# One-hots and weighing of the joined graph-attention stage: two calls a tile pair with two SBUF operands each, or a call per tile with one SBUF operand and a scalar per partition

## The chip, the cores and the metric

The kernel runs on one core of a Trainium2 chip. The metric is the device time of one execution in microseconds (us). About 0.2% (9.4 us) is what a measurement of this kernel can tell from no change.

## The reference, cut to what matters

The model is a node network of 3125 nodes and 53125 edges: an attention layer with 8 heads, a routed expert layer, a graph-attention network of three layers, and a second routed expert layer. The change touches the three graph-attention layers alone. Each does, with 4 heads of 128 columns (layers 1 and 2) or one head of 256 columns (layer 3):

```python
h = (x @ W).reshape(n, heads, out_ch)
e = jax.nn.leaky_relu(al_s[src] + al_d[dst], 0.2)
emax = jax.ops.segment_max(e, dst, num_segments=n)
ee = jnp.exp(e - emax[dst])
denom = jax.ops.segment_sum(ee, dst, num_segments=n)
alpha = ee / (denom[dst] + 1e-16)
out = jax.ops.segment_sum(h[src] * alpha[:, :, None], dst, num_segments=n)
```

## The kernel before

Edges are sorted by destination and cut into 232 items (`ITEMS`) of two tiles of 128 edges, an edge a partition. All edges of an item lead to one tile of 128 nodes. `phase_gat_layer` works on one layer; its engines run written-out loops over the items, in order, and wait on semaphores for each other. For item `t`:

- GpSimd (POOL, L1780) issues two indirect DMAs that gather the rows `h[src]` of the two tiles into slot `t % RING` of `g.rows`. `RING` is 12 slots in layers 1 and 2 and 24 in layer 3. Once the ring is full, an issue waits until item `t - RING` is summed.
- VectorE in `weigh(t)` makes the one-hots `hot` of the destinations (L2022, every fourth item, for four items at once) and multiplies head 0 of the gathered rows by its softmax numerators in `sums(t)` (L2028). In layer 3 head 0 is the whole row.
- ScalarE in `scale(t)` copies the weights beside the row (L1874) and multiplies heads 1 to 3 (L1880, six calls; none in layer 3).
- TensorE in `sum_item(t)` multiplies the one-hots with the rows (L1795) into a bank of PSUM: four matmuls of 261 columns in layers 1 and 2, two of 259 in layer 3. The profile keeps two records of each, so 8 an item and 4.
- VectorE in `add(t - LAG)` adds the bank to the node tile in `acc` (L2051). LAG is 2 in layers 1 and 2 and 5 in layer 3.

Beside this runs the softmax of the next chunk of 64 items (`CH`). For the first 44 items of a chunk three of four also carry `products(q)` on TensorE (L1812, L1815) and `take_scores(q)` on VectorE (L1926, L1930, L1934), as long as there are pairs left: this holds for items 0 to 43, 64 to 107 and 128 to about 155, 116 items in all (the stretches with scores, below). On the last 20 items of a chunk run the 20 steps of `softmax_step`, where TensorE and VectorE take turns. The last 40 items have neither. VectorE's order in a turn is: `weigh(t)`, `take_scores`, a softmax step, `add(t - LAG)`. The order is that of the code; no scheduler moves it.

`sum_item(t)` waits for `marked` (the one-hots), `weighed`, `scaled` and `added` of the bank. Between two gathers GpSimd has a gap that the profile calls issue. At the start of a chunk VectorE rescales `acc` (L2036: `tensor_scalar` with a scalar per partition, in place, on 128 columns in layers 1 and 2 and 256 in layer 3), and at the start of the program it makes `ident` and `before` (L252, L253: `tensor_scalar` on `iota_row` with a scalar per partition).

Of the kernel before, what the change touches and what calls it, by code (L numbers as in the profile page):

```python
# [22 lines left out]
ALU = mybir.AluOpType  # L23
# [3 lines left out]
P = 128  # L27
# [1660 lines left out]
def phase_gat_layer(k, g, s):  # L1688
# [14 lines left out]
    BATCH, HOTS, NB = 4, 3, 4  # L1703
# [22 lines left out]
    with Phase(k, f"gat{g.n}_layer") as ph:  # L1726
# [5 lines left out]
        hot = ph.sb("hot", [P, HOTS, 2 * BATCH, P])  # L1732
# [20 lines left out]

        def heads(t, h0, h1):
            return g.rows[:, t % RING, :, h0 * D:h1 * D].rearrange("p s (h d) -> p s h d", d=D)

        def sums(t):
            return g.sums[:, t // CH % 2, 2 * (t % CH):2 * (t % CH) + 2, :]
# [26 lines left out]
        def _(pe):  # L1785
            def sum_item(t):
                if t % BATCH == 0:
                    pe.wait_ge(marked, t // BATCH + 1)
                pe.wait_ge(weighed, t + 1)
                pe.wait_ge(scaled, t + 1)  # L1790
                if t >= S:
                    pe.wait_ge(added, t - S + 1)
                for p in range(PIECES):
                    for e in range(2):
                        mm = nc.tensor.matmul(k.ps[t % S * PIECES + p][:, 0:PIECE], hot[:, t // BATCH % HOTS, t % BATCH * 2 + e, :],  # L1795
                                              g.rows[:, t % RING, e, p * PIECE:(p + 1) * PIECE], start=(e == 0), stop=(e == 1))
                mm.then_inc(summed, 1)
# [111 lines left out]
        def _(dve):  # L1909
# [106 lines left out]
            def weigh(t):  # L2016
                if t % CH == 0:
                    dve.wait_ge(exped, t // CH + 1)
                if t % BATCH == 0:
                    if t >= HOTS * BATCH:  # L2020
                        dve.wait_ge(summed, t - (HOTS - 1) * BATCH)
                    v.tensor_tensor(hot[:, t // BATCH % HOTS],  # L2022
                                    k.iota_row[:, 0:P].rearrange("p (a n) -> p a n", a=1).to_broadcast([P, 2 * BATCH, P]),
                                    k.dst_in[:, 2 * t:2 * (t + BATCH)].rearrange("p (s a) -> p s a", a=1).to_broadcast([P, 2 * BATCH, P]),
                                    ALU.is_equal).then_inc(marked, 1)
                dve.wait_ge(gathered[t % RING], (t // RING + 1) * 32)
                alpha = sums(t)[:, :, 0:by_dve].rearrange("p s (h o) -> p s h o", o=1)
                v.tensor_tensor(heads(t, 0, by_dve), heads(t, 0, by_dve), alpha.to_broadcast([P, 2, by_dve, D]), ALU.mult  # L2028
                                ).then_inc(weighed, 1)
# [240 lines left out]
```

## Time and profile before

| | |
|---|---|
| median of 3 runs | 4693.39 us (4689.03 to 4693.57) |
| the profiled execution's own time | 4692.36 us |
| its span in the trace | 4690.3 us |
| item loop of layer 1 | 1798 to 2396 us of the span |
| item loop of layer 2 | 2618 to 3216 us |
| item loop of layer 3 | 3389 to 3968 us |
| busy over the span | PE 78%, DVE 58%, ACT 43%, POOL 46% |

The profile is of one execution; its span starts with the first instruction. PE is TensorE, PEld its weight loads, DVE VectorE, ACT ScalarE, POOL GpSimd. The three item loops hold 1775 us, 38% of the span, and only there the changed lines run.

### The profile page before, as it was taken

Reading aid. Unit: us, or ns where it says so; the run is one execution under the profiler, and the core shown is the slowest. Engines: PE = TensorE matmul, PEld = TensorE weight load, DVE = VectorE, ACT = ScalarE, POOL = GpSimd, SP = SyncE. Lnnn points to the kernel's source line nnn. Section 1 sums busy time; section 2 is a strip of 40 time slices with the busy share of each in tenths; the row PEclk is TensorE's granted clock in tenths of the full one; section 3 lists DMA queues with packets and bytes.
Section 4 is the critical chain, followed back from the end, with each engine's and each line's share of the span. In section 5 each row is a group of like instructions: output and inputs, shape, how many; then the busy total and the mean of one; then the engine's idle time right before and its main releaser. Section 6 shows DMA issues by size and latency. Waiting matters only on the chain. (4 is left out here: it accounts for less than half of the span.)

```text
span 4690.3 us, 76158 instructions
## 1 busy us (share of the span) xinstructions
PE 3671.9 (78%) x19902; PEld 2874.6 (61%) x19903; DVE 2735.7 (58%) x6769; ACT 2023.4 (43%) x6613; POOL 2138.2 (46%) x2124
## 2 busy tenths in 40 slices
PE   5788887896999467889768788976677666669995
PEld 3455554785888446677545667755555443458885
DVE  4688888444111458787656878766676655741112
ACT  0588884221222027788743778774311000212221
POOL 0577773001222015777721577772377775012221
PEclk9899998987999788999989899998787666869998
DMA  2677773444778646787643678764555433035555
GB/s 78 186 232 228 231 229 93 152 126 162 260 263 262 163 178 230 243 261 229 195 153 128 234 240 268 229 199 151 171 170 171 132 99 110 10 125 180 187 183 161
DMA packets 348560, 856.05 MB, mean 183 GB/s; under 512 B 52869, under 2 KB 156908, under 8 KB 339692
## 3 DMA queue, kind: packets, MB, share of 16 engines
q0 software_dynamic: 145920, 459.41, 32.6%
q1 hardware_dynamic: 202348, 393.24, 25.2%
q8 instruction: 123, 2.02, 0.2%
q14 instruction: 169, 1.38, 0.1%
HBM read 768.84 MB, written 83.63 MB: 182 GB/s over the span
## 5 line engine op out<-in xcount | busy, mean ns | idle before, releaser
L1780 POOL DMA_INDIRECT h<-h_table,src_of x1392 | 1424.3, 1023 | 954.9 <-PE ps L1815 461.7
L1795 PE MATMUL ps<-h,gat_layer_hot 128*128 128x261 f32 (+1 forms) x4640 | 1308.5, 429 | 372.8 <-DVE h L2028 264.0
L1795 PEld LDWEIGHTS ps<-h,gat_layer_hot 128*128 128x128 f32 x4640 | 910.5, 208 | 644.6 <-DVE gat_layer_hot L2022 208.0
L1880 ACT ACTIVATE h<-h,gat_shared 128x128 f32<-128x128 f32 x2784 | 863.0, 389 | 113.2 <-DMA h<-h_table,src_of 112.8
L727 POOL DMA_INDIRECT edges_rows<-kv_table,src_of x464 | 456.6, 984 | 269.5 <-POOLq L209 128.6
L2051 DVE TENSOR_TENSOR acc<-acc,ps 128x522 f32 (+1 forms) x696 | 421.9, 606 | 238.4 <-issue 105.8
L1012 ACT ACTIVATE acc<-ps,moe_experts_b 128x256 f32<-128x256 f32 x512 | 215.0, 471 | 690.4 <-PE ps L962 690.4
L962 PE MATMUL ps<-moe_experts_turned,moe_experts_w 128*128 128x256 f32 x2048 | 455.4, 381 | 0.0
L2028 DVE TENSOR_TENSOR h<-h,gat_shared 128x256 f32<-128x256 f32 (+1 forms) x696 | 354.7, 510 | 171.3 <-DMA h<-h_table,src_of 169.9
L973 PE MATMUL ps<-moe_experts_w,acc 128*128 128x256 f32 x2048 | 452.1, 379 | 0.0
L973 PEld LDWEIGHTS ps<-moe_experts_w,acc 128*128 128x128 f32 x2048 | 389.1, 190 | 52.9
L962 PEld LDWEIGHTS ps<-moe_experts_turned,moe_experts_w 128*128 128x128 f32 x2048 | 387.1, 191 | 50.5
L1413 POOL DMA_INDIRECT picked_out<-moe_experts_result,moe_slot_out x128 | 125.2, 978 | 635.7 <-DVE moe_experts_result L1390 616.1
L1406 POOL DMA_INDIRECT moe_experts_rows<-normed,moe_slot_in x128 | 124.2, 970 | 630.5 <-POOLq L209 570.2
L791 PE MATMUL ps<-edges_out_rows,h 128*128 128x264 f32 x928 | 280.3, 428 | 86.8 <-DVE edges_out_rows L826 85.1
L1390 DVE TENSOR_TENSOR moe_experts_result<-ps,moe_experts_b 128x512 f32<-128x512 f32 x64 | 44.3, 692 | 483.7 <-PE ps L973 483.7
L1865 ACT COPY gat_layer_of_item<-gat_layer_parts 128x24 bf16 (+1 forms) x696 | 145.7, 218 | 368.8 <-PE ps L1815 183.0
L781 PE MATMUL ps<-h 128*128 x928 | 271.3, 419 | 22.1 <-ACT h L745 13.0
L1812 PE MATMUL ps<-gat_layer_parts,gat_layer_hots 128*128 128x100 bf16 (+1 forms) x4176 | 229.1, 204 | 75.5 <-DMA gat_layer_hots<-hot_table 40.3
L1812 PEld LDWEIGHTS ps<-gat_layer_parts,gat_layer_hots 128*128 128x128 bf16 x4176 | 209.7, 103 | 127.5 <-issue 71.2
L791 PEld LDWEIGHTS ps<-edges_out_rows,h 128*128 128x128 f32 x928 | 174.0, 202 | 177.1 <-DVE edges_out_rows L826 108.1
L781 PEld LDWEIGHTS ps<-h 128*128 128x128 f32 x928 | 174.1, 202 | 98.7 <-issue 76.9
(356 smaller groups left out, 4880.2 us busy)
## 6 DMA issues: line engine op xcount, KB each, us to landing
moe_experts_w<-in_L_ffn_W SPq DMA_DIRECT2D x128, 1024.0 KB
gat_layer_hots<-hot_table SPq DMA_DIRECT2D x174, 562.0 KB
hot_table<-acc SPq DMA_DIRECT2D x58, 562.0 KB
h<-h_table,src_of POOLq DMA_INDIRECT x1392, 2.8
edges_dst_row<-dst_rows SPq DMA_DIRECT2D x58, 256.0 KB, 4.4
acc<-src_rows SPq DMA_DIRECT2D x58, 256.0 KB, 5.7
acc<-dst_rows SPq DMA_DIRECT2D x58, 256.0 KB, 6.5
h_table<-h SPq DMA_DIRECT2D x10, 1280.0 KB
```

What stands on the lines that cost most here:

```text
L727: nc.gpsimd.indirect_dma_start(rows[:, r, s, :], None, k.kv_table, bass.IndirectOffsetOnAxis(ap=k.src_of[:, 2 * t + s:2 * t + s + 1], axis ...
L781: mm = nc.tensor.matmul(psq[r % S][:, s * C:(s + 1) * C], hot_t[:, r % SH, s * P:(s + 1) * P], row(k.h, n, 0, C), start=True, stop=True)
L791: mm = nc.tensor.matmul(pso[r % S][:, 0:W], hot[:, r % S, s * P:(s + 1) * P], out_rows[:, r % S, s, :], start=(s == 0), stop=(s == 1))
L962: mm = nc.tensor.matmul(psh[q][:, j % 2 * GROUP:j % 2 * GROUP + m], f.w1[:, w, b, j * P:(j + 1) * P], f.turned[:, slot, b, 0:m], start=(b ...
L973: mm = nc.tensor.matmul(pso[slot][:, s * C:(s + 1) * C], f.hidden[:, slot, j, s * P:(s + 1) * P], f.w2[:, w, j, :], start=(j == 0), stop=( ...
L1012: last = act.activation(f.hidden[:, slot, j, 0:m], k.ps[2 + q][:, j % 2 * GROUP:j % 2 * GROUP + m], ACT.Gelu, bias=e(j))
L1780: nc.gpsimd.indirect_dma_start(g.rows[:, r, e, 0:W], None, g.table, bass.IndirectOffsetOnAxis(ap=k.src_of[:, 2 * t + e:2 * t + e + 1], axis=0)
L1795: mm = nc.tensor.matmul(k.ps[t % S * PIECES + p][:, 0:PIECE], hot[:, t // BATCH % HOTS, t % BATCH * 2 + e, :], g.rows[:, t % RING, e, p * ...
L1812: nc.tensor.matmul(bank[q % 2][:, i * HT:(i + 1) * HT], one_hot(q, 0, i), parts[:, p, 0:HT], start=(p == 0), stop=(p == 2))
L1880: last = act.mul(cols, cols, sums(t)[:, e, h:h + 1])
L2028: v.tensor_tensor(heads(t, 0, by_dve), heads(t, 0, by_dve), alpha.to_broadcast([P, 2, by_dve, D]), ALU.mult).then_inc(weighed, 1)
L2051: v.tensor_tensor(acc, acc, k.psum[:, t % S * PIECES:t % S * PIECES + PIECES, 0:PIECE], ALU.add).then_inc(added, 1)
```

## The change

The one-hots were one VectorE instruction for four items, which compared two broadcast SBUF operands of 1024 columns. They become two instructions for each item, of 128 columns each, that compare the one SBUF operand `iota_row` with a scalar per partition from `dst_in`. The weighing was one instruction per item with two SBUF operands (the rows, and the weights broadcast along the columns). It becomes one instruction for each of the two tiles, with the rows as the one SBUF operand and the weight as a scalar per partition: 128 columns in layers 1 and 2, 256 in layer 3. The buffer of one-hots keeps its size, 12 items, but is now handed over item by item: TensorE waits for `marked` at each item, and VectorE waits for `summed` of item `t - 12` at each item, where it waited for a group of four.

```diff
-    BATCH, HOTS, NB = 4, 3, 4
+    HOTS, NB = 12, 4
...
-        hot = ph.sb("hot", [P, HOTS, 2 * BATCH, P])
+        hot = ph.sb("hot", [P, HOTS, 2, P])
...
-                if t % BATCH == 0:
-                    pe.wait_ge(marked, t // BATCH + 1)
+                pe.wait_ge(marked, t + 1)
...
-                if t % BATCH == 0:
-                    if t >= HOTS * BATCH:
-                        dve.wait_ge(summed, t - (HOTS - 1) * BATCH)
-                    v.tensor_tensor(hot[:, t // BATCH % HOTS],
-                                    k.iota_row[:, 0:P].rearrange("p (a n) -> p a n", a=1).to_broadcast([P, 2 * BATCH, P]),
-                                    k.dst_in[:, 2 * t:2 * (t + BATCH)].rearrange("p (s a) -> p s a", a=1).to_broadcast([P, 2 * BATCH, P]),
-                                    ALU.is_equal).then_inc(marked, 1)
+                if t >= HOTS:
+                    dve.wait_ge(summed, t - HOTS + 1)
+                for e in range(2):
+                    last = v.tensor_scalar(hot[:, t % HOTS, e, :], k.iota_row[:, 0:P], k.dst_in[:, 2 * t + e:2 * t + e + 1], None,
+                                           ALU.is_equal)
+                last.then_inc(marked, 1)
                 dve.wait_ge(gathered[t % RING], (t // RING + 1) * 32)
-                alpha = sums(t)[:, :, 0:by_dve].rearrange("p s (h o) -> p s h o", o=1)
-                v.tensor_tensor(heads(t, 0, by_dve), heads(t, 0, by_dve), alpha.to_broadcast([P, 2, by_dve, D]), ALU.mult
-                                ).then_inc(weighed, 1)
+                for e in range(2):
+                    for h in range(by_dve):
+                        cols = g.rows[:, t % RING, e, h * D:(h + 1) * D]
+                        last = v.tensor_scalar(cols, cols, sums(t)[:, e, h:h + 1], None, ALU.mult)
+                last.then_inc(weighed, 1)
```

VectorE's instructions in a stretch with scores of layer 1, before, from one `add` to the next but one (`gat1_layer_hot` is `hot`, `h` the gathered rows in `g.rows`, `keys` and `gat_shared` the scores):

```order
L2051 TENSOR_TENSOR acc<-acc,ps 128x522
L2022 TENSOR_TENSOR gat1_layer_hot<-iota_row,dst_in 128x1024
L2028 TENSOR_TENSOR h<-h,gat_shared 128x2x128
L1926 TENSOR_TENSOR keys<-ps,gat1_layer_hots 128x400
L1930 TENSOR_REDUCE gat_shared<-ps 128x4x8
L1934 TENSOR_REDUCE keys<-keys 128x4x4
L2046 TENSOR_LOAD item_tile
L2046 ISA x2
L2051 ISA
L2051 TENSOR_TENSOR acc<-acc,ps 128x522
L2028 TENSOR_TENSOR h<-h,gat_shared 128x2x128
```

The same place in the changed kernel, whose lines stand 3 or 4 lower:

```order
L2048 TENSOR_TENSOR acc<-acc,ps 128x522
L2018 TENSOR_SCALAR gat1_layer_hot<-iota_row,dst_in 128x128 x2
L2025 TENSOR_SCALAR h<-h,gat_shared 128x128 x2
L1922 TENSOR_TENSOR keys<-ps,gat1_layer_hots 128x400
L1926 TENSOR_REDUCE gat_shared<-ps 128x4x8
L1930 TENSOR_REDUCE keys<-keys 128x4x4
L2043 TENSOR_LOAD item_tile
L2043 ISA x2
L2048 ISA
L2048 TENSOR_TENSOR acc<-acc,ps 128x522
L2018 TENSOR_SCALAR gat1_layer_hot<-iota_row,dst_in 128x128 x2
```

Each turn now has four short instructions ahead of the scores, where three of four turns had one and the fourth had two. Nothing else changes its place. On VectorE in layer 3, without scores, the program before has these rows:

```order
L2051 TENSOR_TENSOR acc<-acc,ps 128x259
L2022 TENSOR_TENSOR gat_layer_hot<-iota_row,dst_in 128x1024
L2028 TENSOR_TENSOR h<-h,gat_shared 128x2x256
L2046 TENSOR_LOAD item_tile
L2046 ISA x2
```

And the changed one:

```order
L2048 TENSOR_TENSOR acc<-acc,ps 128x259
L2018 TENSOR_SCALAR gat_layer_hot<-iota_row,dst_in 128x128 x2
L2025 TENSOR_SCALAR h<-h,gat_shared 128x256 x2
L2043 TENSOR_LOAD item_tile
L2043 ISA x2
```

The rows of VectorE's program go from one long comparison in four turns to two short ones in each turn, and the weighing is cut in two.

## Rows read from the trace of the kernel before

**Rows 1.** Layers 1 to 3: stretch, its us, L1780's busy us (count), clock, DMA, GB/s

```profile
1800.00:2390.00 590.00, 452.87 (x440) 0.98 0.76 233
2625.00:3209.00 584.00, 447.26 (x440) 0.98 0.77 236
3403.00:3961.00 558.00, 431.17 (x415) 0.72 0.45 137
```

**Rows 2.** Waits of GpSimd in layer 1: us in total, times, longest

```profile
POOL h L1780 <- issue: 120.6, 396, 0.3
POOL h L1780 <- PE ps L1795: 51.9, 44, 38.5
```

**Rows 3.** The gather's line: duration in ns, least, median, most

```profile
L1780 POOL DMA_INDIRECT h<-h_table,src_of x1392: 940/946/1952, 1733.0 to 3959.4; - x199
```

**Rows 4.** Timeline of GpSimd and VectorE at 2348 us, layer 1: start, length

```profile
2348.53 1.94 POOL L1780 DMA_INDIRECT h<-h_table,src_of  x1 [0.30 <-issue]
...
2348.42 1.22 DVE L2022 TENSOR_TENSOR gat_layer_hot<-iota_row,dst_in 128x1024 f32<-128x1024 f32 x1
```

**Rows 5.** Timeline of both at 3539 us, layer 3, then at 2958 us

```profile
3538.86 0.68 DVE L2028 TENSOR_TENSOR h<-h,gat_shared 128x512 f32<-128x512 f32 x1
3539.26 1.10 POOL L1780 DMA_INDIRECT h<-h_table,src_of  x1 [0.31 <-issue]
3539.46 0.35 DVE L2036 TENSOR_SCALAR acc<-acc,gat_layer_factor  x1
...
2958.39 0.95 POOL L1780 DMA_INDIRECT h<-h_table,src_of  x1 [0.30 <-PE ps L1795]
2958.43 0.96 DVE L2036 TENSOR_SCALAR acc<-acc,gat_layer_factor  x4 [0.58 <-issue]
```

**Rows 6.** Timeline at 1968 us: four short VectorE calls, and a gather

```profile
1968.45 0.87 DVE L2036 TENSOR_SCALAR acc<-acc,gat_layer_factor  x4 [0.23 <-issue]
...
1968.77 0.98 POOL L1780 DMA_INDIRECT h<-h_table,src_of  x1 [0.30 <-PE ps L1795]
```

**Rows 7.** Timeline of VectorE at the start of the program

```profile
1.54 0.29 DVE L252 TENSOR_SCALAR ident<-iota_row,iota_p 128x128 f32<-128x128 f32 x1 [0.31 <-POOL iota_p L243]
1.74 0.28 DVE L253 TENSOR_SCALAR before<-iota_row,iota_p 128x128 f32<-128x128 f32 x1
```

**Rows 8.** Timeline of VectorE, stretch with scores of layer 1

```profile
1853.72 1.22 DVE L2022 TENSOR_TENSOR gat_layer_hot<-iota_row,dst_in 128x1024 f32<-128x1024 f32 x1
1854.86 0.42 DVE L2028 TENSOR_TENSOR h<-h,gat_shared 128x256 f32<-128x256 f32 x1
1855.19 0.57 DVE L1926 TENSOR_TENSOR keys<-ps,gat_layer_hots 128x400 f32<-128x400 f32 x1
...
1862.93 1.22 DVE L2022 TENSOR_TENSOR gat_layer_hot<-iota_row,dst_in 128x1024 f32<-128x1024 f32 x1
```

**Rows 9.** Stretch of layer 1: PE, PEld, DVE, ACT, POOL busy; a row of its waits

```profile
1836.00:1900.00 64.00, 64.00 (x546) 54.67 (x546) 59.07 (x127) 60.15 (x238) 49.39 (x49) 1.00 0.89 295
...
DVE acc L2051 <- PE ps L1795: 2.2, 8, 0.6
```

**Rows 10.** Busy time by stretch, L2028 alone: its count is that of items

```profile
1900.80:1963.70 62.90, 8.38 (x20) 0.95 0.71 210
2194.10:2230.80 36.70, 7.28 (x17) 1.00 0.70 197
2294.90:2392.00 97.10, 16.62 (x39) 1.00 0.65 188
3016.40:3055.40 39.00, 7.36 (x17) 1.00 0.73 206
3120.00:3211.70 91.70, 16.59 (x39) 1.00 0.69 196
```

**Rows 11.** Timeline of ScalarE at 2346 us, no scores

```profile
2346.16 0.19 ACT L1874 COPY h<-gat_shared 128x18 f32<-128x18 f32 x1
2346.98 1.86 ACT L1880 ACTIVATE h<-h,gat_shared 128x128 f32<-128x128 f32 x6 [0.63 <-DMA h<-h_table,src_of]
```

More of the change, by code:

```diff
@@ L1752, in phase_gat_layer @@
         al_s, al_d = g.of_dst[:, 0:H, :], g.of_dst[:, H:2 * H, :]
-        def heads(t, h0, h1):
-            return g.rows[:, t % RING, :, h0 * D:h1 * D].rearrange("p s (h d) -> p s h d", d=D)
         def sums(t):
@@ L1794, in sum_item @@
                     for e in range(2):
-                        mm = nc.tensor.matmul(k.ps[t % S * PIECES + p][:, 0:PIECE], hot[:, t // BATCH % HOTS, t % BATCH * 2 + e, :],
+                        mm = nc.tensor.matmul(k.ps[t % S * PIECES + p][:, 0:PIECE], hot[:, t % HOTS, e, :],
                                               g.rows[:, t % RING, e, p * PIECE:(p + 1) * PIECE], start=(e == 0), stop=(e == 1))
```

## The prediction

> **What bounds the kernel now.** I read the busy times by stretch first, for the gathers alone [rows 1], then who GpSimd waits for [rows 2], then the timeline around single gathers [rows 4 to 6].
>
> In layer 1, 440 gathers take 452.87 us of 590, a mean of 1.029 us [rows 1]. Between them GpSimd has a gap of 120.6 / 396 = 0.30 us that waits for nothing [rows 2], so 440 x 0.30 = 132 us more: 585 of 590. It also shows 44 waits for TensorE, 51.9 us, but 38.5 is the one at the start of the loop, and the other 43 are 13.4 / 43 = 0.31 us each, the same gap. Layer 2 is alike: 447.26 + 132 = 579 of 584. Layer 3: 431.17 + 415 x 0.30 = 556 of 558 [rows 1]. GpSimd's gather queue sets the length of all three item loops.
>
> A gather alone takes 0.945 us (median 946 ns) [rows 3], so its means of 1.029, 1.016 and 1.039 us hold an excess of 0.084, 0.072 and 0.094: 37 + 31 + 39 = 107 us. The timeline shows what it is. A gather begins at 2348.53, and VectorE's comparison L2022 with two SBUF operands runs from 2348.42 to 2349.64; the gather ends at 2350.47, 0.83 us behind it [rows 4]. At 3539.26 the same with L2028: it ends at 3539.54, the gather at 3540.36, 0.82 behind it [rows 5]. So a gather asks for something about 0.945 - 0.82 = 0.125 us into its run, and waits if such a VectorE instruction is under way then. L2022 and L2028, the two lines changed, are what holds it.
>
> The other bound lies close. In the stretch with scores, 1836 to 1900 us, TensorE is busy 64 of 64 us and VectorE 59.07 [rows 9]. VectorE waited for TensorE there for 2.2 us in 8 waits [rows 9], most of it the 0.2 us that it needs for reading the item's tile anyway. From one L2022 to the next are 9.21 us for four items, 2.30 each [rows 8] and some 28 items in the stretch, faster than GpSimd's 2 x 1.33 = 2.66. The ring fills and drains between such stretches and the slow turns of the softmax, 62.90 us for 20 items [rows 10].
>
> **The change, part by part.**
>
> *Durations.* An instruction like the new ones stands in the trace: L252 and L253, `iota_row` against a scalar per partition, 0.28 us long and started 0.20 apart [rows 7]. The in-place scaling L2036 takes 0.87 us for four, so (0.87 - 0.28) / 3 = 0.197 apart [rows 6], and 0.35 long on 256 columns [rows 5].
>
> *VectorE's cost.* Before, from L2022 to the next start is 1.14 us per four items, from L2028 to the next 0.33 [rows 8]: 0.285 + 0.33 = 0.615 an item. After, four starts 0.20 apart: 0.80. So +0.185 an item. Of this some 0.03 is slack (2.2 us over 28 items is 0.08, less the reading of the tile), so +0.15 is exposed where VectorE is level with TensorE. That holds for the 116 items with scores: +17.4 us a layer, in layers 1 and 2. In the softmax turns the one-hots lie on the path between VectorE and TensorE: every second hand-over had 1.14 of L2022, now each has 0.39, and the weighing takes 0.48 to its end for 0.42; (0.39 + 0.06) - 1.14 / 2 = -0.12, ten times a chunk, three chunks: -3 us or so a layer.
>
> *Items without scores.* There VectorE is far from full, and ScalarE is next behind GpSimd: 0.19 + 1.86 us an item [rows 11]. These items went at GpSimd's pace: 17 items in 36.70 and 39 in 97.10 us in layer 1, 17 in 39.00 and 39 in 91.70 in layer 2 [rows 10]. If the ring is full when they begin, they can go at 2.05: 34.9 and 80.0 us. That is -1.8 - 17.1 = -18.9 in layer 1 and -4.1 - 11.7 = -15.8 in layer 2. For this the gathers of the 28 items that 12 full slots leave out of 40 must fit into 80 us: 28 x 2 x 1.27 = 71, they do. The ring will be full, since VectorE's stretches with scores are now slower (2.45 an item) and the gathers faster.
>
> *GpSimd's relief.* I take a gather to be held if a call began more than 0.1 us before it asks: at 2958 the first of four L2036 began at 2958.43, the gather asked at 2958.39 + 0.125, and it kept its 0.95 [rows 5]. Over random phases the excess is the sum of half the squares of the holds over an item's time. Before, layer 1: (1.12^2 / 2 / 4 + 0.32^2 / 2) / 2.6 = 0.080, against 0.084 measured. After: four of 0.18, so 4 x 0.0162 / 2.6 = 0.025. In layer 3: two of 0.18 and two of 0.25, (0.032 + 0.0625) / 2.6 = 0.036. Layer 3 is light on the other engines: saving 415 x (0.094 - 0.036) = 24 us. In layers 1 and 2 the same relief would be 440 x 0.059 = 26 and 440 x 0.047 = 20 us, but there the engines behind the ring take over, as reckoned above.
>
> *The rest.* TensorE's extra wait for `marked` at each item costs nothing: VectorE makes the one-hots just ahead of `weigh`, for which TensorE waited already. VectorE's wait for `summed` of item t - 12 lies nine items behind the work. If the cover fails, each costs VectorE's turn as above. Of the changed lines none lies outside the loops.
>
> *Sum.* Layer 1: 17.4 - 3 - 18.9 = -4.5. Layer 2: 17.4 - 3 - 15.8 = -1.4. Layer 3: -24. Together -30 on the profiled execution's 4692.4, so 4662. The median of the runs, 4693.4, is 1 us above it, which I leave out.
>
> *Bounds.* Starts 0.20 apart is the term that matters. If they overlapped fully with what follows (0.15 us each, nothing exposed) layers 1 and 2 go at GpSimd's new pace. If each took its whole 0.28, see the slower rival. The excess left is between 0 (another 11 + 11 + 15 us off) and what it was.
>
> **A rule weighed against the rows.** In rows 6 four short calls run from 1968.45 to 1969.32, across a gather that asked at 1968.90. The second of them ends at about 1968.93; the gather took 0.98 and was held by 0.04. The third and fourth lay inside it and added nothing. In rows 5 all four lay inside, and it took 0.95. The Trainium skill, page SBUF — State Buffer, section Who interferes with whom, says otherwise: a VectorE call of the kind that `tensor_scalar` becomes there takes the port pair shared with GpSimd for the whole call and blocks it fully, while a call with two SBUF inputs contends only with GpSimd's reads and is thought not to hinder the making of descriptors. By that rule the change would trade calls that do no harm for calls that do. The trace disagrees on both halves: L2022 holds gathers now, and four L2036 inside one did not. By the rows the sum stays; by the rule it is the last rival below.
>
> **The rivals.**
>
> *Full relief, 4622.* VectorE's short calls fit into its gaps, and GpSimd stays the bound in all layers: -26 - 20 - 24 = -70. For it: TensorE, not VectorE, is full at 1836 to 1900. Against: VectorE's 2.30 us an item is the same as TensorE's. Chance 0.13.
>
> *No change, about 4692.* The gathers' relief in layer 3 is eaten in layers 1 and 2: the reading of the item's tile, which now hides behind a long call, shows after short ones. 0.13 us more an item with scores, 232 of them, is 30 us. Chance 0.17.
>
> *Slower: VectorE becomes the bound, 4736.* The calls start as far apart as they are long. With s between starts, an item costs 4s - 0.615 - 0.035 more, the total 232 x that, less 6, 34.7 and 24. It is zero at s = 0.23 us; at 0.28 it is 232 x 0.47 - 65 = +44. Milder, with s = 0.25, +16. For it: VectorE is at 92% in those stretches, and the change makes 16 calls in place of five per four items. Against: both rows that show the spacing have 0.20 [rows 6, 7]. Chance 0.17.
>
> *Slower: short calls hold a gather at any point.* Four of 0.28 an item, of which the gathers' 1.89 of 2.6 us catch 0.8, for 0.17 now: +0.63 x 660 items = +400 us, 5100. Against it the four calls inside a gather in rows 5. Chance 0.03.
>
> *Forecast, 4662*, its own range 4640 to 4682: 0.50.
>
> **How the numbers follow.** Faster by over 0.2% (9.4 us): nearly all of the forecast (0.48), full relief (0.13) and a little of the no-change case (0.04): 0.65. Slower: both slower cases less their mild ends, and the upper edge of no change: 0.18. Same: 0.17. The range goes from full relief, 4622, to 4704, which takes in no change and the mild slower case; above it lies some 0.14, below it 0.04.
>
> **What would show it.** L2025 at 0.28 us and L2018 at 0.28, started 0.20 apart. The gather's mean at 0.97 to 0.98 us in all layers, its most near 1.15 instead of 1.95. VectorE busier at 1836 to 1900, and TensorE with waits for `weighed` or `marked` there. GpSimd with real waits for TensorE (over 0.3 us) in layers 1 and 2, few in layer 3. The last 39 items of layer 1 in about 80 us. Layer 3's loop some 24 us shorter, those of 1 and 2 by 0 to 10. The prediction is wrong if starts are over 0.23 apart, if a gather is held at other points than its first 0.13 us, or if the short calls fall in step with the gathers, so that each is held.

## The result, and the profile after

The changed kernel takes 4653.18 us, the median of 4 runs (4650.92 to 4654.48). The kernel before took 4693.48 beside it (4 runs, 4689.03 to 4695.52). The ratio is 0.9915, with an interval of 0.9898 to 0.9932: 40 us or 0.85% faster. The forecast was 4662.

The page of the changed kernel, first the engines' busy time over its span of 4651.7 us, then three of its costliest groups:

```profile
PE 3654.9 (79%) x19902; PEld 2859.2 (61%) x19903; DVE 2842.2 (61%) x8683; ACT 2015.2 (43%) x6613; POOL 2052.4 (44%) x2124
...
L1777 POOL DMA_INDIRECT h<-h_table,src_of x1392 | 1334.8, 959 | 1003.4 <-PE ps L1811 464.8
L2025 DVE TENSOR_SCALAR h<-h,gat_shared 128x128 f32<-128x128 f32 (+1 forms) x1392 | 393.7, 329 | 58.3 <-DMA h<-h_table,src_of 58.0
L2018 DVE TENSOR_SCALAR gat_layer_hot<-iota_row,dst_in 128x128 f32<-128x128 f32 x1392 | 356.0, 307 | 2.7 <-ACT gat_shared L1884 2.7
```

VectorE is busier (61% for 58%), GpSimd less (44% for 46%), and the kernel is faster. The gathers alone, in the same views as [rows 1] and [rows 3]: by stretch the us, GpSimd's busy us and count, the clock, DMA share and GB/s; then the line's least, median and most in ns.

```profile
1800.00:2390.00 590.00, 423.85 (x440) 0.97 0.76 234
2625.00:3209.00 584.00, 424.78 (x440) 0.97 0.76 236
3395.00:3925.00 530.00, 400.99 (x422) 0.76 0.48 147
```

```profile
L1777 POOL DMA_INDIRECT h<-h_table,src_of x1392: 940/946/1572, 1738.4 to 3923.3; - x199
```

Divide the busy time by the count: 0.963, 0.965 and 0.950 us a gather, for 1.029, 1.016 and 1.039 [rows 1]. Nearly the whole excess over 0.945 is gone. The stretch of layer 3 is 530 us long for 422 gathers, where it was 558 for 415. In layers 1 and 2 the same number of gathers still takes the same 590 and 584 us. The waits of GpSimd say why, in layer 1 and then in layer 3 (us in total, times, longest; as [rows 2]):

```profile
POOL h L1777 <- issue: 124.3, 408, 0.3
POOL h L1777 <- PE ps L1791: 70.5, 32, 37.9
```

```profile
POOL h L1777 <- issue: 124.3, 408, 0.3
POOL h L1777 <- PE ps L1791: 5.2, 17, 0.3
```

In layer 3 the wait for TensorE is never longer than the usual gap of 0.3 us, so GpSimd still never waits. In layer 1, less the one of 37.9 at the start of the loop, 32.6 us in 31 waits are left, a mean of 1.05 us. There the ring was full: the gathers are no longer the bound.

Each loop from its first item's ScalarE copy to its last add, and the excess, which is the sum of (duration - 0.945) over its 464 gathers:

| | layer 1 | excess | layer 2 | excess | layer 3 | excess | rest of the span |
|---|---|---|---|---|---|---|---|
| before | 601.0 | 37 | 595.7 | 31 | 575.9 | 40 | 2917.7 |
| after | 595.5 | 8 | 596.0 | 9 | 537.5 | 2 | 2922.7 |

The loops give -5.5, +0.3 and -38.4 us, together -43.6. In layer 3 the excess alone fell by 37.9 us, and GpSimd had no other wait there before or after: the whole gain of that loop is the gathers' own shorter time. The rest of the span, where nothing was changed, is 5 us longer; a second profile of the kernel before has 2914.1 there, so a few us of that part vary from one execution to the next.

**What VectorE pays.** Its busy time in the stretch of [rows 9], and the wait in which TensorE now stands there:

```profile
1836.00:1900.00 64.00, 61.18 (x520) 50.88 (x518) 59.55 (x187) 54.91 (x217) 48.46 (x52) 1.00 0.88 295
```

```profile
PEld ps L1791 <- DVE gat_layer_hot L2018: 3.6, 6, 1.0
```

TensorE has gone from 64.00 busy of 64 to 61.18, waits for one-hots, and gets through fewer instructions (520 for 546). The weighing alone by stretch, as in [rows 10] (here an item has two, so 72 are 36 items): the stretch with scores from item 8 to 43 of layer 1, then its last 39 items, its 17 items without scores, and the last 39 of layer 2. The row ahead of them is the same 36 items in the kernel before.

```profile
1817.60:1900.90 83.30, 15.08 (x36) 1.00 0.88 292
...
1823.10:1912.90 89.80, 18.10 (x72) 1.00 0.88 297
...
2312.80:2391.30 78.50, 20.00 (x79) 1.00 0.72 205
...
2218.60:2248.10 29.50, 8.83 (x34) 1.00 0.73 208
...
3133.60:3211.20 77.60, 19.78 (x79) 1.00 0.71 206
```

Where there are scores the items have become slower: 89.8 / 36 = 2.494 us for 83.3 / 36 = 2.31. Where there are none they have become faster: 78.3 us from weighing to weighing for 97.1 in layer 1, 77.4 for 91.7 in layer 2, and 29.5 for 36.7 over the 17 items. Layers 1 and 2 are a trade between these two, and it comes out near zero. Layer 3 has only the gain.

**Where the excess of layer 3 went.** Timeline of GpSimd and VectorE in layer 3 of the changed kernel (start, length, count; in brackets the idle time ahead):

```profile
3850.80 0.95 POOL L1777 DMA_INDIRECT h<-h_table,src_of  x1 [0.30 <-issue]
3851.06 0.80 DVE L2025 TENSOR_SCALAR h<-h,gat_shared 128x256 f32<-128x256 f32 x2 [0.91 <-DMA h<-h_table,src_of]
3851.89 0.42 DVE L2048 TENSOR_TENSOR acc<-acc,ps 128x259 f32 x1
3852.05 0.94 POOL L1777 DMA_INDIRECT h<-h_table,src_of  x1 [0.30 <-issue]
3852.23 0.48 DVE L2018 TENSOR_SCALAR gat_layer_hot<-iota_row,dst_in 128x128 f32<-128x128 f32 x2
3853.30 0.95 POOL L1777 DMA_INDIRECT h<-h_table,src_of  x1 [0.30 <-issue]
3853.60 0.77 DVE L2025 TENSOR_SCALAR h<-h,gat_shared 128x256 f32<-128x256 f32 x2 [0.89 <-DMA h<-h_table,src_of]
```

A gather asks 0.125 us into its run, at 3850.93 and 3852.18. The weighing starts at 3851.06, when its rows land, and the one-hots at 3852.23: both just behind the point. An item takes 3853.30 - 3850.80 = 2.50 us, exactly two gathers, and since VectorE waits for the rows of a gather, it stays in step with them. At neither point is one of the changed calls under way. The `add` that is (3851.89 to 3852.31) reads PSUM and one SBUF operand, and the gather keeps its 0.94. Over layer 3, once the ring is full, 24% of the gathers had a changed call under way at that point, where these calls fill 48% of the time; in layers 1 and 2 it is 37 and 39% for 36%, as by chance.

**What was not foreseen: VectorE waits too.** Timeline of a stretch with scores of layer 1:

```profile
1855.37 0.94 POOL L1777 DMA_INDIRECT h<-h_table,src_of  x1 [0.30 <-issue]
1856.61 0.94 POOL L1777 DMA_INDIRECT h<-h_table,src_of  x1 [0.30 <-issue]
...
1855.47 0.48 DVE L2018 TENSOR_SCALAR gat_layer_hot<-iota_row,dst_in 128x128 f32<-128x128 f32 x2
1855.87 0.56 DVE L2025 TENSOR_SCALAR h<-h,gat_shared 128x128 f32<-128x128 f32 x2
1856.35 0.68 DVE L2048 TENSOR_TENSOR acc<-acc,ps 128x522 f32 x1
1856.95 0.66 DVE L2018 TENSOR_SCALAR gat_layer_hot<-iota_row,dst_in 128x128 f32<-128x128 f32 x2
1857.34 0.52 DVE L2025 TENSOR_SCALAR h<-h,gat_shared 128x128 f32<-128x128 f32 x2
```

The pair at 1855.47 takes 0.48 us, as two calls 0.20 apart should. The pair at 1856.95 takes 0.66: its second call began at about 1857.15, 0.54 us into the gather of 1856.61, and did not end before the gather was over at 1857.55. The line of the one-hots in layer 1 shows how far it goes (least, median, most, in ns):

```profile
L2018 DVE TENSOR_SCALAR gat_layer_hot<-iota_row,dst_in x464: 272/281/537, 1798.0 to 2389.5; 128x128 f32<-128x128 f32 x155
```

By where in a gather these calls began, in layer 1: 0.45 to 0.60 us in, a mean of 0.46 us; 0.60 to 0.675 in, 0.37; 0.675 to 0.75 in, 0.32; at any other point 0.28. The gather itself stays at 0.945. The calls with two SBUF operands do not show it: the 32 weighings before that began 0.45 to 0.675 us into a gather of layer 1 took 0.42 us each, as usual.

### The profile page after: what moved, and what is told of

It reads as the page before. It is cut to its first block and busy times, and to the rows that moved or that the text cites. A ratio compares the mean times of both kernels' runs of the same rounds, so it can differ in the third digit from the quotient of the medians.

```text
span 4651.7 us, 78586 instructions
## 1 busy us (share of the span) xinstructions
PE 3654.9 (79%) x19902; PEld 2859.2 (61%) x19903; DVE 2842.2 (61%) x8683; ACT 2015.2 (43%) x6613; POOL 2052.4 (44%) x2124
## 3 DMA queue, kind: packets, MB, share of 16 engines
q8 instruction: 125, 2.05, 0.2%
## 5 line engine op out<-in xcount | busy, mean ns | idle before, releaser
L1777 POOL DMA_INDIRECT h<-h_table,src_of x1392 | 1334.8, 959 | 1003.4 <-PE ps L1811 464.8
L1791 PE MATMUL ps<-h,gat_layer_hot 128*128 128x261 f32 (+1 forms) x4640 | 1284.8, 423 | 346.0 <-DVE h L2025 233.7
L2025 DVE TENSOR_SCALAR h<-h,gat_shared 128x128 f32<-128x128 f32 (+1 forms) x1392 | 393.7, 329 | 58.3 <-DMA h<-h_table,src_of 58.0
L2018 DVE TENSOR_SCALAR gat_layer_hot<-iota_row,dst_in 128x128 f32<-128x128 f32 x1392 | 356.0, 307 | 2.7 <-ACT gat_shared L1884 2.7
```

The lines of the kernel that those rows point to most:

```text
L1777: nc.gpsimd.indirect_dma_start(g.rows[:, r, e, 0:W], None, g.table, bass.IndirectOffsetOnAxis(ap=k.src_of[:, 2 * t + e:2 * t + e + 1], axis=0)
L2018: last = v.tensor_scalar(hot[:, t % HOTS, e, :], k.iota_row[:, 0:P], k.dst_in[:, 2 * t + e:2 * t + e + 1], None, ALU.is_equal)
L2025: last = v.tensor_scalar(cols, cols, sums(t)[:, e, h:h + 1], None, ALU.mult)
```

## The experiments

All diffs are against the changed kernel. The first four put the form of before back in some layers or for one of the two lines.

**One fact on the times first.** The twelve runs were made at four occasions, each on another chip. At three of them the kernel before took about 5142 to 5147 us, in the last 4694, as in the result above. All comparisons are with the kernel before at the same occasion. What differs between the occasions is told after the first group, since it turned out to decide what the change is worth.

### New form in one layer, or for one line

Layer 3 alone, layers 1 and 2 alone (a condition in each):

```diff
+        def short_hots(t):
+            return H == 1          # layers12_only: H > 1
+        def short_weigh(t):
+            return H == 1          # layers12_only: H > 1
...
+                if short_hots(t):
...
+                elif t % 4 == 0:
+                    if t >= HOTS:
+                        dve.wait_ge(summed, t - HOTS + 4)
+                    v.tensor_tensor(hot[:, t % HOTS:t % HOTS + 4].rearrange("p t s n -> p (t s) n"),
...
+                                    ALU.is_equal).then_inc(marked, 4)
```

> New form in layer 3 alone, layers 1 and 2 as before. If the gain is the gathers that are no longer held where they pace a whole loop: layer 3's loop some 38 us shorter, gather mean there 0.95 us, loops 1 and 2 unchanged, total about 4656 us (-37). If the gain were spread over all layers: clearly less, -15 to -25.

> New form in layers 1 and 2 alone. By the prediction's steps VectorE's longer turn with scores eats what the faster gathers give: loops 1 and 2 within 6 us of before in sum, total 4687 to 4693 us. Within them the stretches with scores go at about 2.49 us an item (before 2.31) and the last 39 items in 80 us or less (before 97 and 92). A rival, that short calls are as good for these layers, would want -20 or more.

One-hots alone in the new form (`short_hots` always, `short_weigh` never), and weighing alone (the reverse):

> One-hots in the new form, weighing in the old one, all layers. L2022 held gathers for 25, 21 and 23 us, L2028 for 9, 8 and 17. If holds decide: layer 3 some 21 us shorter; in layers 1 and 2 VectorE's extra is 0.1 us an item with scores (+11 a layer), the last items go near 2.05 us: -8 to -12 each. Total about 4652 us. If instead the shorter path from landing to TensorE gave the gain, the one-hots, which are made ahead of the landing, would give nothing in layer 3.

> Weighing in the new form, one-hots in the old one, all layers. If holds decide: layer 3 some 17 us shorter, layers 1 and 2 about even (VectorE +0.06 us an item with scores, 9 and 8 us of holds less), total about 4675 us. If the path from landing to TensorE decides: layer 3 takes nearly the whole 38 us, total about 4655 us.

Measured, with the kernel before at 5142.57 us (24 runs, 5131.44 to 5160.14):

| | median us | ratio | layer 1, excess | layer 2, excess | layer 3, excess |
|---|---|---|---|---|---|
| layer3_only | 5158.45 | 1.0029 [1.0016, 1.0042] | 702, 27 | 698, 33 | 636, 2 |
| layers12_only | 5151.19 | 1.0022 [1.0011, 1.0034] | 706, 11 | 714, 10 | 630, 50 |
| hots_only | 5158.60 | 1.0042 [1.0028, 1.0056] | 700, 12 | 709, 15 | 635, 15 |
| weigh_only | 5151.83 | 1.0017 [1.0001, 1.0033] | 707, 26 | 703, 20 | 623, 29 |

The gathers did what the theory says in all four. Their line in layer 3, in this order:

```profile
L1786 POOL DMA_INDIRECT h<-h_table,src_of x424: 940/947/1293, 3779.8 to 4415.9; - x142
```

```profile
L1786 POOL DMA_INDIRECT h<-h_table,src_of x425: 940/947/1962, 3780.3 to 4430.1; - x142
```

```profile
L1786 POOL DMA_INDIRECT h<-h_table,src_of x420: 940/946/1622, 3779.8 to 4413.0; - x140
```

```profile
L1786 POOL DMA_INDIRECT h<-h_table,src_of x424: 940/947/1957, 3779.7 to 4418.5; - x142
```

A gather of 1.96 us is there when the 1.22 us comparison is (second and fourth), and gone with it. With the 0.69 us weighing left (third) the most is 1.62. The most that a gather takes follows the longest call that is left in the layer.

The times did not follow, and all four runs missed the times that were expected of them. No part was faster; the excess of layer 3 fell by 48 us from the second kernel to the first, and its loop became 6 us longer. It is longer with the one-hots in the new form (635 and 636) than without (623 and 630); the new weighing does not lengthen it (630 to 623, 635 to 636). Each of these is one profile, and loops of one layer with the same code differ by up to 6 us among these runs, so neither the 6 us nor the split between the lines is clear of that. The next run repeats the changed kernel.

### The changed kernel again

No edit.

> The changed kernel once more, unaltered, as a measure of the chip that this call gets. The seven runs ahead of it were made on a chip where the kernel before takes 5142 us, not 4693, and where each of them, whatever part of the change it holds, is 0.2 to 0.6% slower than before. If the two chips differ in what bounds the loops: 4653 us (0.9915 of before) on a chip where before takes 4693; 5155 to 5165 us (1.003) where it takes 5142, with gaps of GpSimd behind TensorE and issue gaps of all engines, though the gathers are as short as here.

Measured: 5167.12 us for 5142.40 (14 runs of before), ratio 1.0037 [1.0021, 1.0054]. Here the very kernel of the result above is slower than before. Its gathers in layer 3 and GpSimd's waits there (busy and mean; idle by releaser, where remote is one that the profile cannot name; then us in total, times, longest):

```profile
L1777 POOL DMA_INDIRECT h<-h_table,src_of x416 | 395.3, 950 | 236.8 <-issue 106.8 <-PE ps L1791 75.2 <-remote 54.8
```

```profile
POOL h L1777 <- issue: 106.8, 346, 1.1
POOL h L1777 <- PE ps L1791: 75.2, 40, 21.2
POOL h L1777 <- remote: 54.8, 30, 4.2
```

The gathers are as short as before (0.950 us), but GpSimd now waits 75 us for TensorE, up to 21 at a time, where in the result above it waited 5.2 in 17 gaps of 0.3. The gathers' pace is not the bound at these occasions, so freeing them brings nothing. That the 0.4% lost is then the price of VectorE's extra calls is argued, not shown. What else is different shows stage by stage. Here is the attention layer's pass over the edges, which the change does not touch, in the kernel before at the occasion of the result and then in this run (stretch, us, then busy us and count of PE, PEld, DVE, ACT and POOL, clock, DMA share, GB/s):

```profile
152.00:764.00 612.00, 514.43 (x1856) 348.06 (x1856) 521.84 (x1159) 503.98 (x1391) 459.37 (x463) 0.93 0.74 222
```

```profile
152.00:912.00 760.00, 545.61 (x1856) 396.14 (x1856) 526.61 (x1158) 500.87 (x1390) 469.90 (x463) 0.82 0.61 179
```

By TensorE's first and last instruction in a stage, this pass takes 760 us for 616 in the result's profile, and the three graph-attention stages 779, 779 and 722 for 660, 661 and 589. Everything else in the program takes 2121 to 2131 us in all fourteen profiles of both conditions. So the 513 us of difference lie in the four stages that go over the edges item by item, whether they are hardware loops (the attention pass) or written out (the other three); written-out dense stages are not slower. The granted clock is lower as well: 0.68 in this run's layer 3 loop (3800 to 4440 us) for 0.76 in the result's profile, and the median matmul of `sum_item` there takes 0.64 us for 0.46.

Some of the added time is idle time of about 0.70 us. Gaps of 0.66 to 0.74 us between two records of an engine, waiting instructions counted as records, number 113 on VectorE, 79 us, and 70 on TensorE with its weight loads, 49 us; in the profile of the result they are 10 and 11, 7 and 8 us. Most of them, 104 and 58, lie in the attention pass. The profiles of the slower occasions also hold only about half of the semaphore updates (31,288 here, 58,726 in the result's profile of the same kernel), so that an idle time that they put down to issue or remote can be a wait whose end was not recorded. What sets these conditions stays open. They came with the occasion, and so with the chip, and held for all kernels of it. No profile of the kernel before was taken in the slower condition.

### What holds a gather: the kind of operands or the length

Both of these kernels add to the changed one, in every fourth item of layer 3, a VectorE call of 1024 columns whose result nothing reads (the work of the reference is all done; the call is extra). The first has two SBUF operands, the second is a reduction with one:

```diff
+                if H == 1 and t % 4 == 0:
+                    if t:
+                        dve.wait_ge(spared, t // 4)
+                    v.tensor_tensor(spare[:], k.iota_row[:, 0:P]...to_broadcast([P, 8, P]),
+                                    k.dst_in[:, 2 * t:2 * t + 8]...to_broadcast([P, 8, P]),
+                                    ALU.is_equal).then_inc(spared, 1)
...
+                    # spare_reduce, in its place:
+                    v.tensor_reduce(spare[:, :, 0], k.iota_row[:, 0:P]...to_broadcast([P, 8, P]),
+                                    AX.X, ALU.add).then_inc(spared, 1)
```

> The changed kernel with one more VectorE call every fourth item of layer 3: the old comparison of 1024 columns with two SBUF operands, into columns that nothing reads. If a call with two SBUF operands holds the gathers: gather mean in layer 3 from 0.95 back to about 1.0 us, its most near 1.9 us, +20 us on the changed kernel's 4653, about 4673. If VectorE's time decides, the same as the run with the reduction beside it.

> The changed kernel with one more VectorE call every fourth item of layer 3 that takes as long (a reduction of 1024 columns, some 1.2 us) but has one SBUF operand; nothing reads its output. If only two SBUF operands or a short tensor_scalar hold a gather: gather mean stays at 0.95 us and the time at 4653 to 4658. If VectorE's time decides: as much longer as the run with the comparison.

The two calls in ns, and the gathers of layer 3, first of the one, then of the other:

```profile
L2026 DVE TENSOR_TENSOR gat_shared<-iota_row,dst_in x58: 1205/1215/1221, 3799.2 to 4440.8; 128x1024 f32<-128x1024 f32 x58
...
L1779 POOL DMA_INDIRECT h<-h_table,src_of x416 | 415.0, 998 | 216.4 <-issue 111.1 <-PE ps L1793 74.9 <-remote 30.3
```

```profile
L2026 DVE TENSOR_REDUCE gat_shared<-iota_row x58: 1201/1212/1221, 3806.9 to 4449.0; 128x8 f32<-128x1024 f32 x58
...
L1779 POOL DMA_INDIRECT h<-h_table,src_of x416 | 398.2, 957 | 235.5 <-issue 108.1 <-PE ps L1793 94.1 <-remote 33.4
```

The extra calls are equally long (1.215 and 1.212 us). With two SBUF operands the excess over layer 3's gathers is 22.0 us and the longest gather 2.08 us; with one it is 5.2 us and 1.32, near the 2.2 of the kernel without either. In each kernel 32 gathers of layer 3 began with the extra call under way: with two SBUF operands their mean excess is 0.446 us, with one 0.006. So of two calls of one length, the one with two SBUF operands holds gathers and the reduction does not. The times were 5173.15 us, ratio 1.0042 [1.0025, 1.0059], and 5182.14, 1.0062 [1.0043, 1.0081]: the holds cost nothing there, since the gathers were not the bound.

### Old form in the turns with scores, new form elsewhere

```diff
+        def short_hots(t):
+            return H == 1 or scored(4 * (t // 4)) is None
+
+        def short_weigh(t):
+            return H == 1 or scored(t - 2) is None
```

> Layer 3 and the items without scores of layers 1 and 2 in the new form, items with scores there in the old form. If VectorE's longer turn is what eats the gain in layers 1 and 2: stretches with scores at 2.31 us an item as before, last items as in the changed kernel; layer 1 and 2 some 15 us shorter each than before, layer 3 38 us: total about 4625 us. If the old calls' holds on the gathers matter there after all: about 4640 to 4650 us.

> Layer 3 and the items without scores of layers 1 and 2 in the new form, the items with scores there in the old one. On a chip where before takes 4693: if VectorE's longer turn eats the gain in layers 1 and 2, about 4625 us; if holds by the old calls matter in the stretches with scores, 4640 to 4650. Where before takes 5142: about 5160 again.

Measured: 5165.21 us for 5147.32, ratio 1.0038 [1.0023, 1.0053], and again 5167.07 for 5142.40, ratio 1.0041 [1.0024, 1.0058]. Beside the changed kernel (5167.12) that is no difference. What was expected of it at 4693 us stays untested: both runs belong to the occasions of 5142 us and more, and nothing follows for the other: this version was not run where the kernel before takes 4694.

### At the occasion of 4694 us: hand-over and length apart

The kernel before again, for a second profile of it:

> The kernel before, unaltered, for its trace under the conditions of these runs (5142 us). If the item loops here are no longer paced by the gathers: gathers held as in the first trace (some 30 to 50 us in each layer), yet real waits of GpSimd for TensorE, loops of some 700, 700 and 620 us. If they are paced by them: waits of GpSimd of 0.3 us alone, as in the first trace.

It was meant to show the slower condition and met the faster one. It took 4686.13 us in one run, and layer 3's gathers were again held:

```profile
L1780 POOL DMA_INDIRECT h<-h_table,src_of x395 | 411.2, 1041 | 120.3 <-issue 113.6 <-PE ps L1795 6.4 <-PE ps L1815 0.3
```

Short calls, but eight at a time every fourth item, as the old form hands over:

```diff
-                for e in range(2):
-                    last = v.tensor_scalar(hot[:, t % HOTS, e, :], ...
-                last.then_inc(marked, 1)
+                if t % 4 == 0:
+                    if t >= HOTS:
+                        dve.wait_ge(summed, t - HOTS + 4)
+                    for e in range(8):
+                        last = v.tensor_scalar(hot[:, t % HOTS + e // 2, e % 2, :], k.iota_row[:, 0:P],
+                                               k.dst_in[:, 2 * t + e:2 * t + e + 1], None, ALU.is_equal)
+                    last.then_inc(marked, 4)
```

> The changed kernel, but with its short one-hot calls made eight at a time, every fourth item, and handed over as a group. Same calls, same lengths. If the hand-over at each item is what makes the changed kernel slower here: back to before or under it, 5140 to 5150 us. If it is the number of calls: 5160 to 5170 us, as the changed kernel. Where before takes 4693: 4650 to 4660 us by either, gathers held for under 5 us in layer 3.

And the reverse: one long comparison of two SBUF operands and 256 columns for each item, handed over item by item; the weighing as in the changed kernel.

```diff
-                for e in range(2):
-                    last = v.tensor_scalar(hot[:, t % HOTS, e, :], ...
-                last.then_inc(marked, 1)
+                v.tensor_tensor(hot[:, t % HOTS],
+                                k.iota_row[:, 0:P].rearrange("p (a n) -> p a n", a=1).to_broadcast([P, 2, P]),
+                                k.dst_in[:, 2 * t:2 * t + 2].rearrange("p (s a) -> p s a", a=1).to_broadcast([P, 2, P]),
+                                ALU.is_equal).then_inc(marked, 1)
```

> The changed kernel with its two short one-hot calls of an item joined to one comparison of 256 columns with two SBUF operands, handed over at each item. If the number of calls costs: 5145 to 5155 us here; if the hand-over at each item does: 5160 to 5170 us. Gathers in layer 3 held for some 9 us, between the changed kernel's 2.3 and the 29 us of the run with the old one-hots, since a hold of 0.3 us costs far less than one of 1.1.

Measured, with the kernel before at 4693.60 us (9 runs, 4684.23 to 4702.26):

| | median us | ratio | layer 1, excess | layer 2, excess | layer 3, excess |
|---|---|---|---|---|---|
| kernel before, second profile | | | 597.0, 33 | 598.2, 34 | 574.7, 39 |
| changed (the result's profile) | 4653.18 | 0.9915 [0.9898, 0.9932] | 595.5, 8 | 596.0, 9 | 537.5, 2 |
| hots_grouped | 4680.18 | 0.9970 [0.9958, 0.9983] | 610.8, 8 | 609.2, 6 | 540.8, 6 |
| hots_long_by_item | 4642.75 | 0.9890 [0.9873, 0.9906] | 591.0, 12 | 588.9, 12 | 540.9, 5 |

Gathers of layer 3 from 3395 to 3925 us, of hots_grouped, then of hots_long_by_item:

```profile
L1777 POOL DMA_INDIRECT h<-h_table,src_of x420 | 402.4, 958 | 128.0 <-issue 116.7 <-PE ps L1791 10.4 <-PE ps L1811 1.0
```

```profile
L1777 POOL DMA_INDIRECT h<-h_table,src_of x410 | 391.9, 956 | 124.9 <-issue 119.4 <-PE ps L1791 5.5
```

In none of the last three does a changed line make a call of two SBUF operands longer than the 0.42 us weighing of before (the softmax keeps a few of 0.69 and 1.07 us), and all have short gathers and the same layer 3 within 3.4 us, whatever form the one-hots have. In layers 1 and 2 they part. Grouped calls cost 15 and 13 us more than the same calls spread over the items, and hots_grouped missed the 4650 to 4660 us that were expected either way. The waits of TensorE for them at 1836 to 1900 us:

```profile
PEld ps L1791 <- DVE gat_layer_hot L2019: 6.1, 6, 1.3
...
PE ps L1791 <- DVE gat_layer_hot L2019: 3.9, 6, 0.9
```

That is 10.0 us, where the changed kernel has 3.6 and the 0.6 of this row:

```profile
PE ps L1791 <- DVE gat_layer_hot L2018: 0.6, 1, 0.6
```

A run of eight calls stands in front of the first item that needs one of them, and the ring of one-hots is no help where TensorE already waits for VectorE. That this is the whole of the 15 us is argued from these rows, not shown.

The long comparison by item is the fastest version that was run, 10 us ahead of the changed kernel, though the two intervals just overlap. Its excess in layer 3, 5 us, is under the 9 that were expected. Its line in all three layers:

```profile
L2017 DVE TENSOR_TENSOR gat_layer_hot<-iota_row,dst_in x696: 408/419/491, 1794.9 to 3912.2; 128x256 f32<-128x256 f32 x174
```

It takes 0.42 us at nearly every call, and its successor starts 0.33 behind it. Two short calls take 0.39 where nothing holds them, and more where a gather does. A stretch with scores takes 88.0 us for 36 items, between the 83.3 of before and the 89.8 of the change. For this it holds gathers a little more: 12 for 8 and 9 us of excess in layers 1 and 2, where they have slack, and 5 for 2 in layer 3. The weighing alone, or the change in one layer alone, was not run in this condition; what each is worth here is read from the stretches above, not from runs.

## Why the prediction was right, and where it was off

**Right: the gathers' pace bounded all three loops, and the long calls were what stretched it.** Every kernel without the 1.22 us comparison lost its 1.95 us gathers; spare_sbuf brought them back with one such call and spare_reduce, with a call as long, did not. The point near the start holds too: in the trace before, 129 comparisons of 1.22 us began 0.05 to 0.85 us into a gather and none lengthened it by more than 0.012 us, and where one was under way from the gather's start the gather ended 0.819 us behind it (median of 130; the same for 141 weighings). The weighing against the rule was right in what it meant for the sum: short calls inside a gather do not lengthen it. It read the rule by half, though, as the last section tells.

**Off by 14 us: "over random phases the excess is the sum of half the squares", layer 3.** It gave 0.036 us left per gather and a saving of 24; measured are 0.005 and 38.4 us. The phases are not random: a changed call is under way at half as many asking points as chance would give (24% for 48%). In layer 3 VectorE waits for the rows, so its calls fall in step with the gathers, and in the timeline above they lie just behind the point where one asks. The text named only the bad case of this, that each call would be held in step. That they lie on the good side here is shown by the timeline and the count; that they would in another kernel is not. The formula was checked against layer 1 alone, where it gave 0.080 for 0.084. With the 0.69 us weighing of layer 3 it gives (1.12^2 / 2 / 4 + 0.59^2 / 2) / 2.6 = 0.127 for the 0.094 of before: the phases were not random there to begin with, and the rows at hand could have said so.

**Off by 0.03 us an item: VectorE's cost.** The working had +0.185 of which +0.15 exposed; +0.18 an item was measured over items 8 to 43. Two things go into it. The slack of 0.03 that was taken off was not kept: TensorE waits for one-hots instead. And "L2025 at 0.28 us and L2018 at 0.28" failed as a mean, 0.301 and 0.308, because a gather under way holds the short calls that start 0.45 to 0.67 us into it. On L2018 in layer 1 that is (0.308 - 0.281) x 464 = 12.5 us, of which only the part in stretches with scores can count. Over all items with scores from item 8 on, the stretches grew by 18.9 and 19.3 us in layers 1 and 2, for 17.4 predicted. How much of the miss is the holding and how much the slack was not measured apart.

**Right within 3 us, in part by luck: layers 1 and 2 as a trade.** Predicted were -4.5 and -1.4 us, measured from weighing to weighing -5.0 (597.9 to 592.9) and +0.9 (592.5 to 593.4). The trade is as forecast, but its terms missed on both sides and cancelled. The items with scores cost 18.9 and 19.3 us for 17.4, the softmax turns +0.6 and +4.4 for -3, the first eight items +1.3 and +0.9 for nothing, and the items without scores gave -25.9 and -23.7 for -18.9 and -15.8. In these last ones ScalarE is the next bound, as named, but at another price. On the 17 items of layer 1 it has no idle time:

```profile
2213.70:2245.30 31.60, 31.58 (x103) 1.00 0.73 209
```

That is 31.6 / 17 = 1.86 us an item, for the 0.19 + 1.86 = 2.05 of the working, which added up lengths although each call starts before the one ahead of it has ended. On the last items it is busy 90% and still waits 7.9 us for gathers, 2.10 us an item between its copies; there the 80.0 came near the measured 78.3 and 77.4 by two errors that offset each other.

**"TensorE's extra wait for `marked` costs nothing"** was too little said. The hand-over by item is worth 15 and 13 us against the grouped one once the calls are short. The prediction counted no loss for it, rightly, but no gain either, because it compared with a single call of 1.14 us.

**The rivals.** Full relief (4622) fell: VectorE does become late in the stretches with scores. No change and VectorE as the bound fell here: starts are 0.20 apart, not 0.25. Yet at the other occasions the kernel is 0.4% slower than before, with gathers held as little. The prediction had no case for an execution in which the gathers are not the bound.

**Gather means.** Forecast 0.97 to 0.98 us everywhere with a most near 1.15; measured 0.963, 0.965 and 0.950, with a most of 1.57 us over all and 1.08 in layer 3. The few long ones in layers 1 and 2 are held by calls of the softmax with two SBUF operands, which the prediction left out and the change did not touch:

```profile
2125.80 1.07 DVE L1980 TENSOR_TENSOR gat_shared<-gat_layer_work,is_last 128x512 f32<-128x512 f32 x1
```

```profile
2126.01 1.56 POOL L1777 DMA_INDIRECT h<-h_table,src_of  x1 [0.30 <-issue]
```

Of the 8 us of excess left in layer 1 they make 2.7, with six gathers; the short calls of the change make 3.5, with 48.

The 43.6 us of the loops became 38.6 of the span and 40 of the median, because the unchanged rest was 5 us longer in this profile. The spread of that part between the two profiles of before, 3.6 us, is nearly as large. So of the 9 us between the forecast and 4653, layer 3 makes 14 and the longer rest takes 5 back.

## What to carry to other kernels

When a DMA queue that GpSimd feeds sets the pace, compare its instruction's median with its mean: here 0.946 and 1.03 us, and the difference, 107 us over three loops, was VectorE calls that lay over one point of it. Cut the long calls with two SBUF operands down, for by the formula that fitted layer 1 what a hold costs grows with the square of the call, but cut no further than needed: one call of 0.42 us gave nearly the same relief as two of 0.28 and cost VectorE less. Hand such a result over in the piece that the consumer needs next, and price the extra calls only where that engine is the late one; where the queue is not the bound, the same change costs 0.4%.

## What the runs showed of the hardware

- A gather of 128 rows asks for something at one point near its start. With a VectorE call of two SBUF operands under way there, it ends 0.82 us after the call does (up to 1.95 us for 0.945); one that begins 0.05 us or more behind the gather's start does not lengthen it (129 comparisons). An equally long reduction with one SBUF operand does not hold it (0.006 us of mean excess for 0.446, 32 gathers each). A short `tensor_scalar` under way there does: five weighings of the changed kernel begun 0.10 to 0.15 us ahead of a gather lengthened it by 0.09 us on average, and it again ended 0.82 us behind them.
- The reverse also happens: a `tensor_scalar` of 128 columns that begins 0.45 to 0.67 us into a gather takes up to 0.54 us instead of 0.28 and ends 0.05 us behind the gather, which is not lengthened. The Trainium skill, page SBUF — State Buffer, section Who interferes with whom, says that calls of this kind contend with GpSimd over a shared port pair, and that whichever of the two issues first keeps it for its whole instruction while the other is blocked. The prediction told this for VectorE first alone, and took calls inside a gather that did not lengthen it as speaking against the rule; for a gather that issues first, the rule has VectorE wait, and so it does here. The trace does not agree that it is for the whole instruction: the 168 one-hots of layer 1 that began in the first 0.45 us of a gather took 0.28 us each. The page also says that a call with two SBUF inputs is thought not to hinder the making of descriptors; the 22.0 us of spare_sbuf speak against it.
- There are conditions, the same for all kernels of an occasion, in which the four stages that go over the edges are 18 to 23% longer (779 for 660 us in layer 1, 722 for 589 in layer 3, 760 for 616 in the attention pass, the changed kernel both times) while the rest of the program is as fast as ever. Their cause stays open. They turned 0.85% faster into 0.4% slower.
